# Reordered weight preparation and separate load semaphores in a gated-recurrence plus feed-forward layer

## The reference

```
def attn(x, W_r, W_i, lambd):             # on layernorm(x); W_r, W_i are 1024x1024
    r = sigmoid(x @ W_r.T); i = sigmoid(x @ W_i.T)
    log_a = 8.0 * r * log_sigmoid(lambd)
    a = exp(log_a)
    b = sqrt(max(1 - exp(2*log_a), 0)) * (i * x)
    h_t = a_t * h_(t-1) + b_t             # associative scan over the 2048 positions
    return h
def ffn(x, W_fc, ln_w, ln_b, W_proj):     # on layernorm(x); W_fc 4096x1024, W_proj 1024x4096
    # absmean(W) = sign(Ws) * min(round(|Ws|), 1), Ws = W / (mean|W| + 1e-6)
    h = gelu(x @ absmean(W_fc).T)
    h = layernorm(h, ln_w, ln_b)          # over the 4096
    return h @ absmean(W_proj).T
x = x + attn(layernorm(x)); x = x + ffn(layernorm(x))
```

## Time and profile before

| | us |
|---|---|
| median of 2 runs | 2222.32 (2221.03 to 2223.62) |
| the profiled execution, whole | 2225.87 |
| its span, from the first to the last instruction, slowest core | 2224.2 |
| spans of the eight cores | 2206.4 to 2224.2 |
| busy in the span: TensorE matmuls / VectorE / ScalarE / GpSimd | 1488.2 / 1018.8 / 619.4 / 313.1 |

### The profile page before, as it was taken

One profiled execution on the slowest core, in us unless ns is written; L12 is line 12 of the kernel. 1 busy time (PEld: TensorE's weight loads), 2 busy tenths in 40 slices (PEclk: granted clock), 3 DMA queues, 4 the chain that ended last, 5 costly groups with the idle time before them and its releaser, 6 DMA issues.

```text
span 2224.2 us, 20120 instructions; the slowest of 8 cores (2206.4 to 2224.2 us)
## 1 busy us (share of the span) xinstructions
PE 1488.2 (67%) x6052; PEld 612.9 (28%) x6052; DVE 1018.8 (46%) x1457; ACT 619.4 (28%) x1013; POOL 313.1 (14%) x308
## 2 busy tenths in 40 slices
PE   0353007755949676885869594959496768868697
PEld 0011002212314232332324142424142323323243
DVE  1435646644661455325641655146624553256413
ACT  0184221111423133222422242214221332224220
POOL 1221213421110111001110111011101110021100
PEclk9776558876979888897979697969797888979799
DMA  7475886651402131212221132014021312122114
GB/s 196 143 236 182 260 265 185 174 127 54 135 15 100 48 100 52 104 48 66 86 104 36 41 123 80 25 56 134 17 98 48 100 52 104 48 66 86 66 33 129
DMA packets 103745, 223.67 MB, mean 101 GB/s; under 512 B 34516, under 2 KB 34516, under 8 KB 103640
## 3 DMA queue, kind: packets, MB, share of 16 engines
q1 hardware_dynamic: 91352, 178.34, 25.2%
q0 software_dynamic: 12288, 44.05, 7.1%
HBM read 192.98 MB, written 29.37 MB: 100 GB/s over the span
## 4 chain that ended last, share of the span: by engine, by line
PE 60%; DVE 16%; DMA 10%; ACT 6%; issue 6%; POOL 1%; DVEq 0%; SPq 0%; ACTq 0%; POOLq 0%
PE pY L485 21%; PE pool L769 20%; DMA xb<-wfct 5%; PE pool L618 5%; PE pool L629 3%; PE pS L755 2%; PE pQ L757 2%; DVE tmp L588 2%; DVE ln_bf L590 2%; DVE tmp L284 2%; DVE ln_bf L286 2%; PE pS L459 2%; DMA wp_sc<-qn_buf 2%; PE pQ L460 2%; DMA xb<-wrt 1%
## 5 line engine op out<-in xcount | busy, mean ns | idle before, releaser
L769 PE MATMUL pool<-ln_bf,wfc_q 128*128 128x512 bf16 x2048 | 511.5, 396 | 100.2 <-DVE ln_bf L286 100.2
L485 PE MATMUL pY<-g_sb,wp_sl 128*128 128x512 bf16 x2048 | 467.6, 389 | 57.3 <-DVE tmp L507 41.0
L769 PEld LDWEIGHTS pool<-ln_bf,wfc_q 128*128 128x128 bf16 x2048 | 207.4, 102 | 373.8 <-issue 151.4
L485 PEld LDWEIGHTS pY<-g_sb,wp_sl 128*128 128x128 bf16 x2048 | 203.8, 100 | 314.5 <-issue 85.0
L777 ACT ACTIVATE g_sb<-pool 128x512 bf16<-128x512 f32 x256 | 152.8, 598 | 451.7 <-PE pool L769 451.6
L784 DVE TENSOR_TENSOR gsq<-g_sb 128x512 bf16<-128x512 bf16 x224 | 95.3, 425 | 390.0 <-ACT g_sb L777 377.6
L618 PE MATMUL pool<-ln_bf,wr_sl 128*128 128x512 bf16 x512 | 143.3, 430 | 113.7 <-DVE ln_bf L590 113.7
L653 ACT ACTIVATE t_r<-pool 128x512 f32<-128x512 f32 x64 | 38.0, 593 | 374.4 <-PE pool L618 374.4
L588 POOL TENSOR_TENSOR t_r<-xb,rs_t 128x512 f32<-128x512 f32 x16 | 25.6, 1599 | 761.4 <-DVE mb_t L469 760.2
L629 PE MATMUL pool<-ln_bf,wi_sl 128*128 128x512 bf16 x512 | 127.5, 394 | 0.0
L676 DVE SCALAR_TENSOR_TENSOR t_q<-t_a 128x512 f32<-128x512 f32 x64 | 44.2, 691 | 176.6 <-ACT t_a L664 176.6
(11 more groups left out here) (120 smaller groups left out, 1726.7 us busy)
## 6 DMA issues: line engine op xcount, KB each, us to landing
wp_sl<-wp_sc SPq DMA_DIRECT2D x128, 512.0 KB, 4.1
xb<-x SPq DMA_DIRECT2D x8, 2048.0 KB, 9.0
wr_sl<-wr_sc SPq DMA_DIRECT2D x64, 256.0 KB, 2.6
wi_sl<-wi_sc SPq DMA_DIRECT2D x64, 256.0 KB, 3.0
xb<-wfct SPq DMA_DIRECT2D x32, 512.0 KB, 6.4
xb<-wfct POOLq DMA_DIRECT2D x32, 512.0 KB, 6.1
y<-xb SPq DMA_DIRECT2D x8, 2048.0 KB, 7.6
t_q<-wpt POOLq DMA_DIRECT2D x16, 512.0 KB, 4.7
```

Of the source, the lines that this page charges most:

```text
L485: fn = lambda E, kh=kh, sl=sl, bank=bank, first=(kh == 0), last=last: E.matmul(pY[bank][:, :], wp_sl[:, sl * 2048 + (kh % 16) * 128: sl * ...
L769: fn = lambda E, h=h, d=d, bank=bank: E.matmul(pool[bank][:, :], wfc_q[:, d * H + h * 128: d * H + h * 128 + 128], lnch(d), start=(d == 0) ...
```

## The change

Three edits:

1. The cast stage interchanges its loops: piece kd of W_r, then piece kd of W_i, then kd+1. The slot becomes (2 kd + widx) % 4. The staging half and the issuing engine of a load still follow kd % 2, while the scatter's engine follows the slot's parity and so follows the matrix: SP for W_r, POOL for W_i. The token of each scatter is kept, and `emit_wri_load` waits for the 8 scatters of W_r before a slice of W_r, and for the 8 of W_i before a slice of W_i.
2. The W_proj loads of the middle preparation get semaphores of their own, d_stg4 on SP and d_stg5 on POOL.
3. The W_proj loads of `emit_prep2b_load` use the same two.

```diff
-              "d_stg0", "d_stg1", "d_stg2", "d_stg3", "d_y"):
+              "d_stg0", "d_stg1", "d_stg2", "d_stg3", "d_stg4", "d_stg5", "d_y"):
...
-    for widx, (WSRC, WSC) in enumerate(((WRT, wr_sc), (WIT, wi_sc))):
-        for kd in range(ND):
-            slot = (widx * ND + kd) % 4
+    tok_wsc = {}
+    for kd in range(ND):
+        for widx, (WSRC, WSC) in enumerate(((WRT, wr_sc), (WIT, wi_sc))):
+            slot = (kd * 2 + widx) % 4
             st = stg0 if kd % 2 == 0 else stg1
             qeng = "sync" if kd % 2 == 0 else "gpsimd"
             usewait(qeng, ("stg", kd % 2))
...
             src2 = qn_s(slot).rearrange("p (ke j) -> p ke j", ke=ND)
-            emit_scatter(slot, dst, src2)
-    tok_wrsc = list(sc_last.values())
-    tok_wisc = []
+            tok_wsc[(widx, kd)] = emit_scatter(slot, dst, src2)
...
             tl2 = b.emit(qeng2, lambda E, st2=st2, i=i:
-                         E.dma_start(st2, WPT[128 * i:128 * (i + 1), :]), inc=f"d_stg{sl}", n=16)
+                         E.dma_start(st2, WPT[128 * i:128 * (i + 1), :]), inc=f"d_stg{4 + sl % 2}", n=16)
...
         p2b_loads[i] = b.emit(qeng, lambda E, st=st, i=i:
-                              E.dma_start(st, WPT[128 * i:128 * (i + 1), :]), inc=f"d_stg{sl}", n=16)
+                              E.dma_start(st, WPT[128 * i:128 * (i + 1), :]), inc=f"d_stg{4 + sl % 2}", n=16)
...
-        for t_ in tok_wrsc:
-            b.wait("sync", t_)
+        for kd2 in range(ND):
+            b.wait("sync", tok_wsc[(0, kd2)])
...
-        for t_ in tok_wisc:
-            b.wait("sync", t_)
+        for kd2 in range(ND):
+            b.wait("sync", tok_wsc[(1, kd2)])
```

## The result

The changed kernel took 2240.7 us in the median of 11 runs, against 2225.0 for the kernel before, measured beside it. The ratio is 1.0071, 95% interval 1.0056 to 1.0086: **15.7 us slower**, 14 forecast. It is inside the 2% and well clear of no change. Ratios, here and in the experiments, leave out the executions in which one die ran longer at a lower clock, so they can differ from the quotient of two medians. The slowest core changed, from core 3 to core 4, so I read both.

The account below looks back on a forecast made before the run. The prediction took the last-ending wait of each preparation stage as the bound, with the last cast on the path. Terms +22 - 8 + 0 = +14 us took the median from 2222.3 to 2236 us, range 2216 to 2252.

Parts of the forecast that it names:

- Edit 1, the chain: Cast stage: waits across SP's and POOL's lists make 13 landings in a row in place of 8; 21.8 us fixed.
- Edit 1, the size: Cast stage, first to last cast: 76.4 us against 54.3, a cost of 22 us, bounds 14 and 30.
- the lone landing: Cast stage: a load with no second load beside it lands in 4.3 us, bounds 3.7 and 5.0; nine such.
- Edit 2: Middle preparation: W_fc issue hidden, 0.55 x 12 = 6.6 us, and stream starting up to 6.1 earlier; 8 us gained, bounds 0 and 13.
- the cap of 265: Middle preparation: at 265 GB/s, the highest slice mean, 28.95 MB takes 109 us and not 120, 11 us gained.
- Edit 3 at nothing: W_proj preparation: load i+2 waiting for load i on the same engine costs 0 us.
- the finer waits at nothing: Waits of `emit_wri_load` gain nothing: slices are wanted only at the first matmul, 33.6 us after the last cast.
- The slack of 1.6 us on POOL: W_proj preparation: POOL's closest loads are 5.61 us apart and the first takes 4.0, leaving 1.6 us that covers the wait.
- A: Cast stage: DMA engines set it, landings shrink with fewer in flight, issue order is free; time 2214 us; chance 12%.
- B: Middle preparation gains 13 us or a little more, cast stage costs only 14; time 2223 us; chance 13%.
- C: Middle preparation gains nothing, lone loads in the cast stage take 4.3 to 5.0 us; time 2244 to 2252 us; chance 20%.
- D: W_proj preparation: held-back loads hold scatters in 8 rounds, 30 us beyond the 14, slower by over 2%; chance 3%.

Follow-up runs that it names:

- e4_wide_scatter: The changed kernel with W_r/W_i scratch laid out so scatters write whole 2 KB rows, slice loads reading 256-byte runs; ratio 1.0066 to the kernel before.

## Why the prediction was right, point by point

- **Edit 1, the chain.** Right in form: 13 landings in a row. This is the chain of waits of core 4 in the changed kernel (start us, us, what; the DMA pieces alone):

```profile
5.45 11.62 DMA xb<-wrt
18.40 6.14 DMA xb<-wit
26.99 5.74 DMA xb<-wrt
34.15 7.44 DMA xb<-wit
43.60 5.89 DMA xb<-wit
51.86 4.87 DMA xb<-wrt
58.23 6.34 DMA xb<-wit
66.63 5.62 DMA xb<-wit
74.63 4.76 DMA xb<-wrt
80.90 6.42 DMA xb<-wit
89.37 5.35 DMA xb<-wit
97.10 4.66 DMA xb<-wrt
103.26 4.67 DMA xb<-wit
```

  Thirteen pieces, with the predicted pattern of pair, SP, POOL. The first cast starts at 17.16 and the last at 108.09. Taking the 12 landings' 67.9 us from these 90.9 leaves 23.0 fixed, and every other core gives 23.0 too; the prediction had 21.8.
- **Edit 1, the size.** The mis-sized term is above all the lone landing: 4.3 taken, 5.3 on core 4, 4.9 on core 3 and 5.0 over all cores measured (means of nine), with 6.7, 5.9 and 6.1 paired where 5.3 was taken. The stage took 86.8 us in the mean, not 76.4. Of these 10.4 us the lone landings make 6.8, the paired 2.5 and the fixed part 1.2. The last cast moved by 30.4, not 22, at the upper bound named, and at 104.2 us it lies outside the 86 to 102 given as a sign. The step that failed is the choice of the earlier trace rows as nearest row because "there too a scatter runs beside the load". Without the small runs (`e4_wide_scatter`) the cores show 4.3 lone, 5.4 paired and 21.3 fixed, nearly the terms of the prediction. But the scatters beside the earlier trace rows were in 256-byte runs as well, so those runs alone don't tell the two rows apart; POOL's lone loads with one scatter took 4.6 on core 3 where the earlier trace rows has 4.0. The rest of that difference stays open.
- **Edit 2.** Gain 8 predicted, 11.1 measured (between thresholds and first W_proj piece), within 0 to 13. Landings did grow on core 3, from 6.1 to 7.3 for POOL's loads of W_fc (235 to 350 us), and the rate of the stage rose from 257 to 285 GB/s: the cap of 265, taken from the earlier trace rows, was too low. The 0.55 in the product is an issue of 0.53, which makes 6.4 and not 6.6.
- **Edit 3 at nothing, the finer waits at nothing.** Right: the W_proj preparation isn't longer, the layernorm block is 33.2 us in both. Load 0 beside x took 14.10 on core 4, where 11.14 was taken, and VectorE waited 0.19 us for load 2 behind it. The slack of 1.6 us on POOL was not always there: on core 3 its loads waited for the W_proj load before them, 5.3 us in 5 waits and 4.6 in one, and the stage got no longer.
- **The sum.** +22 - 8 = +14 against +15.7. The two misses, +8.4 and -3.1 with another -2.2 in the W_proj preparation, cancel in part: that the total was closer than its terms is luck. With the rest, which moved by 1.3 though nothing was changed in it, the marks add up to 18.5 and the two profiled executions are 18.6 apart, where the runs' ratio gives 16.
- **The rivals.** A fell: landings didn't halve as the engines emptied to 51%. The Trainium skill's rule ("DMA: Bandwidth & Descriptors", "Issuing engines are not separate DMA queues"), read strictly, would have made the change nearly free, as it says that issuing from several engines saves only the sequencer's time. The trace differs: the same transfers from the same two engines took 87 us and not 55 once each list had to wait for casts of the other's pieces, and there the measurement decides. Whether one issuing engine could fill the DMA engines, no run here shows. B's middle gain was nearly there, but not its cheap cast stage; C had the cast stage nearly right (22 to 30) and the middle wrong. D fell: 39.4 us of waits for scatters on core 3, 46.4 before.

## What to carry to other kernels

When two lists of instructions each issue loads and stores, write both lists out and follow which wait stands in front of which load: giving a load to one list and its store to another turned 8 rounds into 13, though no transfer was added. Read DMA share together with the stage's length: 51% in a stage that only moves and casts data was here the sign of a chain of waits, and more loads in flight helped although each became slower. Undo the parts of a mixed change one at a time; here a change that lost 0.7% held one part worth 0.7% and another that cost 1.5%.

## What the runs showed of the hardware

- A 512 KB load with no second load but one or two scatters beside it landed in 4.6 to 5.4 us (medians of core 3), at 132 to 139 GB/s and 51 to 52% busy over the stage; with four loads in flight a load took 7 to 10 us, at 271 GB/s and 95% busy. The slower landings made the faster stage.
- Writing 256 KB in 256-byte runs took 3.0 us instead of 2.2 and made the load beside it up to 1.0 us slower, yet with four loads in flight the last cast moved only from 56.5 to 58.6 us. On POOL, issuing such a write took 0.91 us instead of 0.55.
